# A layer's combination inside the second attention's loop, and a ternary layer's weight preparation moved ahead of the first experts

## The chip, the cores and the metric

The kernel runs on one core of a Trainium2 chip. The metric is device microseconds of one execution; the kernel before took 1500.44 us in the median of three runs (1497.56 to 1501.2). The core's engines are TensorE (PE), VectorE (DVE), ScalarE (ACT), GpSimd (POOL) and SyncE (SP, which here only starts DMAs). Each engine runs its own instructions in order and waits for others on semaphores.

## The reference

Four decoder layers on x of 64 x 64 x 128 float32 (4096 tokens, 32 tiles of 128 tokens x 128 features). Each layer has a cross-attention and a feed-forward part, both on a normalised x and both gated and added. The change touches the end of layer 0 and layer 1:

```
x = x + tanh(g_xattn[0]) * L0_xattn(layernorm(x), ctx, mask)      # 16 heads
x = x + tanh(g_ffn[0])   * L0_ffn(layernorm(x))                   # 16 experts, one per token
x = x + tanh(g_xattn[1]) * L1_xattn(layernorm(x), ctx, side)      # 16 heads, bias per head
x = x + tanh(g_ffn[1])   * L1_ffn(layernorm(x))                   # ternary weights

# L1_ffn: absmean(W) = sign(W/g) * min(round(|W/g|), 1), g = mean|W| + 1e-6
h = gelu(x @ absmean(W_fc).T)          # 128 -> 512
h = layernorm(h) * ln_w + ln_b
out = h @ absmean(W_proj).T            # 512 -> 128
```

"Combination" below is the second line's sum: the experts' output rows, times each token's gate, are added to x. Layers 2 and 3 follow and are not touched.

## The kernel before

x stays in SBUF as 32 tiles (core.x). The program is a sequence of phases; between phases all engines meet at a barrier. The functions return one program for each engine, and a phase queues them one behind another on that engine.

The phase `attentions_and_experts` holds three stages that follow each other without a barrier: `first` (attention of layer 0 with the router that sends each token's row to an expert's table in DRAM), `expert` (16 experts, each 256 rows: rows and weights are loaded, transposed, multiplied, and the results scattered to a table `rows_out`) and `second` (attention of layer 1). On PE and DVE the queue is first, expert, second; on SP too, with the rows of `rows_out` loaded into `got` by `FirstCombine.load_rows` after all results are stored.

Both attentions come from `attention16_programs`. Every engine runs a loop over i from -5, and a stage of the pipeline works on tile i plus some lead. For a tile: ACT normalises it (xn, L485) with rstd and nmr = -mean*rstd; PE transposes xn and projects q, k, v (L386 to L399); ACT copies them out (L500 to L508); POOL spreads kT into a block form kbd (L341), adds a shift to x (L357) and in the second attention adds the mask to the bias tile (side_add, L350); PE multiplies the scores (L413); DVE adds the bias to the scores (`masked`, L583), takes maxima (L590), subtracts them (`centred`, L598); ACT takes exponents (L515); PE transposes them (L428) and multiplies with v (L440); DVE divides (L607, L610), and after PE's output product (L454) adds to x (`residual`, L618) and takes bn_stats of the new x (L625). Buffers of kbd, xn and q are double; side tiles have four buffers; the scores have one.

The second attention gets `added`, a `FirstCombine`: before DVE's loop it calls `fresh(t)` for t = 0 to 31. fresh multiplies got by the gate and adds it to x (L1740, one instruction), takes bn_stats of the tile before (L1747), and after each group of 8 tiles runs `root_on_vector` (L199 to L219): 18 small DVE instructions that give mean, rstd (three Newton steps) and nmr of the group. ACT's xn of tile t waits for the nmr of its group. Only then does DVE enter its loop, whose first work is masked(0).

The next phase is `ternary_ffn` (l1f). SP loads W_fc, W_proj, ln_w and ln_b, then fills a table of layer 2 with empty rows (34 transfers, L1949). DVE computes the roots of all 32 tiles, and then prepares the weights: sums of absolute values (L2064), thresholds, signs (L2076 to L2079), gains and gate (L2081, L2083), and with PE's help (L1982, L1985, L1989) a shift and the correction for the mean (L2085, L2088). Then its loop over tiles starts with `normalise` (L2094).

Of the kernel before, what the change touches and what calls it, by code (L numbers as in the profile page):

```python
# [37 lines left out]
class Core:  # L38


    def __init__(self, nc, ctx):
# [10 lines left out]
        self.gates = sb("gates", [P, 8])  # L52
        self.tables = {}
# [131 lines left out]
def statistics(nc, ph, core, name="", groups=1):  # L185
# [8 lines left out]
    def on_vector(dve, group=0):  # L194
        V = nc.vector
        at = slice(group * NT // groups, (group + 1) * NT // groups)
        done = group * (8 + 3 * ROOT_STEPS)
# [23 lines left out]
        dve.wait_ge(nmr_ready, group + 1)  # L221
# [3 lines left out]
def attention16_programs(nc, core, ph, gate, w_dram, b_dram, neg_steps, side=None, fills=(), routing=None, added=None):  # L225
# [94 lines left out]
    def gpsimd(pool):  # L320
# [223 lines left out]
    def vector(dve):  # L544
# [3 lines left out]
        V.memset(fill_rows[:, :, 0:D], 0.0).then_inc(s["fill_ready"], 1)  # L548
        V.memset(fill_rows[:, :, D:ROW], NOWHERE).then_inc(s["fill_ready"], 1)
# [12 lines left out]
        def fresh(t):  # L562
# [1156 lines left out]
class FirstCombine:  # L1719
# [5 lines left out]
    def __init__(self, nc, core, ph, r):  # L1725
# [3 lines left out]
        self.s = {n: ph.sem(n) for n in ("added", "summed")}  # L1729
# [13 lines left out]
    def moments(self, dve, t):  # L1743
# [1415 lines left out]
```

## Time and profile before

| | us |
|---|---|
| median of three runs | 1500.44 (1497.56 to 1501.2) |
| the profiled execution's own time | 1497.47 |
| its span, first to last instruction | 1495.7 |
| PE busy (matmul) | 1155.3 (77%) |
| DVE busy | 986.8 (66%) |
| POOL busy | 834.0 (56%) |
| ACT busy | 788.1 (53%) |
| mean granted clock of TensorE | 0.892 of full |

Times in views are microseconds from the span's start. The stages that the change touches lie there as follows: first attention from about 27, experts from about 260, second attention from about 325, ternary layer from about 538 to 640. A timeline row has the start, the duration, the engine, the line, the operation, output<-inputs, a count, and in brackets how long the engine stood before it and what released it. Rows of consecutive instructions of one kind may be merged; then the duration is that of the merged piece.

### The profile page before, as it was taken

The page shows a single profiled execution, that of the slowest core. Times are in us where ns is not written, and L with a number is a line of the kernel's source. Part 1 is how long each engine was busy: PE and PEld are TensorE (multiplying, and loading weights), DVE is VectorE, ACT ScalarE, POOL GpSimd, SP SyncE. Part 2 cuts the span into 40 slices and gives each one's busy share as a digit, 9 for nine tenths or more (in the row PEclk, how much of TensorE's full clock was granted, in tenths as well). Part 3 has the DMA queues.
Part 4 walks back from the last instruction along what each step waited for, and adds up shares of the span by engine and source line. Part 5 has one row for each costly group of instructions (what it writes and reads, how often), then busy time and mean ns, then how long its engine had stood idle before and what let it go on. Part 6 is the DMA issues. An engine that isn't in the chain of part 4 may idle for free.

```text
span 1495.7 us, 38800 instructions
## 1 busy us (share of the span) xinstructions
PE 1155.3 (77%) x12350; PEld 974.5 (65%) x12350; DVE 986.8 (66%) x3128; ACT 788.1 (53%) x2054; POOL 834.0 (56%) x1103
## 2 busy tenths in 40 slices
PE   2888883962888859968529996698888973999991
PEld 1676662951767637736529996476666662999991
DVE  3788982239899957768834434588777864555554
ACT  2677761421788825545417776576555541433333
POOL 0356766442677703373764554677888874333334
PEclk9999995985899969987559999799999995999996
DMA  5222331570223257060116777200000301777765
GB/s 148 89 103 98 97 97 39 175 210 20 105 101 114 73 219 294 1 189 24 53 58 195 206 212 211 77 2 6 16 17 16 104 21 55 219 240 232 238 207 172
DMA packets 144386, 177.72 MB, mean 119 GB/s; under 512 B 18986, under 2 KB 94268, under 8 KB 144192
## 3 DMA queue, kind: packets, MB, share of 16 engines
q1 hardware_dynamic: 133504, 154.22, 33.1%
q0 software_dynamic: 10688, 21.06, 4.0%
q8 instruction: 105, 1.72, 0.5%
q14 instruction: 89, 0.73, 0.2%
HBM read 119.16 MB, written 57.23 MB: 118 GB/s over the span
## 4 chain that ended last, share of the span: by engine, by line
PE 31%; POOL 8%; DVE 7%; issue 6%; ACT 3%; DMA 2%; POOLq 0%; SPq 0%; DVEq 0%; ACTq 0%
PE l3e_ps_h L1604 4%; PE l2e_ps_h L1604 4%; PE l3e_ps_h L1606 4%; PE l3e_ps_y L1615 4%; PE l2e_ps_y L1615 4%; POOL l_rows_in L1178 3%; PE l3a_ps_kv L2628 2%; PE l3a_ps_ym L2699 2%; POOL l3a_cms L2521 1%; PE l3a_ps_q L2612 1%; DVE x L706 1%; POOL l3a_nvt L2538 1%; POOL l3a_qc L2529 1%; PE l3a_ps_kv L2603 1%; PE l3e_ps_x L1596 1%
## 5 line engine op out<-in xcount | busy, mean ns | idle before, releaser
L1645 ACT ACTIVATE l3e_sT<-l3e_ps_h 128x128 f32<-128x128 f32 x284 | 78.8, 278 | 134.2 <-PE l3e_ps_h L1606 121.3
L1698 POOL DMA_INDIRECT l_rows_out<-l3e_y,l3e_target x71 | 69.0, 972 | 137.8 <-DVE l3e_y L1680 133.7
L1656 DVE TENSOR_TENSOR l3e_hT<-l3e_sT,l3e_ps_h 128x128 f32<-128x128 f32 x284 | 81.7, 288 | 85.4 <-ACT l3e_sT L1645 75.8
L1642 ACT ACTIVATE l2e_hT<-l2e_ps_h,l2e_b1c 128x128 f32<-128x128 f32 x284 | 104.5, 368 | 56.1 <-PE l2e_ps_h L1604 39.8
L1604 PE MATMUL l2e_ps_h<-l2e_xT,l2e_w 128*128 128x128 f32 x568 | 111.0, 279 | 0.4 <-DVE l2e_xT L1669 0.4
L1604 PE MATMUL l3e_ps_h<-l3e_xT,l3e_w 128*128 128x128 f32 x568 | 111.0, 277 | 0.5 <-DVE l3e_xT L1669 0.5
L1606 PE MATMUL l3e_ps_h<-l3e_xT,l3e_w 128*128 128x128 f32 x568 | 110.6, 277 | 0.0
L1615 PE MATMUL l3e_ps_y<-l3w_w,l3e_hT 128*128 (+1 forms) x568 | 109.3, 275 | 0.0
L1615 PE MATMUL l2e_ps_y<-l2e_w,l2e_hT 128*128 (+1 forms) x568 | 109.2, 275 | 0.0
L1698 POOL DMA_INDIRECT l_rows_out<-l2e_y,l2e_target x71 | 69.1, 973 | 70.2 <-DVE l2e_y L1678 56.8
L1604 PEld LDWEIGHTS l3e_ps_h<-l3e_xT,l3e_w 128*128 128x128 f32 x568 | 87.1, 194 | 0.7 <-DVE l3e_xT L1669 0.7
L1604 PEld LDWEIGHTS l2e_ps_h<-l2e_xT,l2e_w 128*128 128x128 f32 x568 | 86.9, 194 | 0.9 <-DVE l2e_xT L1669 0.9
L1606 PEld LDWEIGHTS l3e_ps_h<-l3e_xT,l3e_w 128*128 128x128 f32 x568 | 87.1, 194 | 0.0
L1615 PEld LDWEIGHTS l2e_ps_y<-l2e_w,l2e_hT 128*128 128x128 f32 x568 | 86.1, 192 | 0.0
L1178 POOL DMA_INDIRECT l_rows_in<-l2a_rt_rows,l2f_slot x64 | 63.2, 988 | 40.9 <-ACT l2a_rt_rows L1020 23.2
L1615 PEld LDWEIGHTS l3e_ps_y<-l3w_w,l3e_hT 128*128 128x128 f32 x568 | 86.0, 192 | 0.1
L350 POOL TENSOR_TENSOR l1a_side<-l1a_side,l1a_neg 128x1024 f32<-128x1024 f32 x32 | 75.8, 2368 | 0.0
L1178 POOL DMA_INDIRECT l_rows_in<-l3a_rt_rows,l3f_slot x64 | 64.7, 1011 | 19.1 <-issue 17.4
L341 POOL TENSOR_TENSOR l1a_kbd<-l1a_kT,l1a_own 128x512 f32<-128x512 f32 x32 | 33.3, 1041 | 74.4 <-ACT l1a_kT L502 74.4
L341 POOL TENSOR_TENSOR l0a_kbd<-l0a_kT,l0a_own 128x512 f32<-128x512 f32 x32 | 34.5, 1077 | 56.5 <-ACT l0a_kT L502 56.2
L1966 POOL TENSOR_TENSOR l1f_rs<-l1f_ve,l1f_half 128x1 f32<-128x1 f32 x32 | 17.7, 552 | 66.6 <-DVE x L2113 45.5
L428 PE MATMUL l1a_ps_t<-ident,l1a_p 128*128 128x128 f32 x256 | 41.7, 288 | 16.2 <-ACT l1a_p L515 16.0
(551 smaller groups left out, 3766.4 us busy)
## 6 DMA issues: line engine op xcount, KB each, us to landing
l3e_w<-in_L_ffn_W SPq DMA_DIRECT2D x142, 256.0 KB
l2e_w<-in_L_ffn_w SPq DMA_DIRECT2D x79, 256.0 KB, 4.6
l_rows_in<-l1f_empty SPq DMA_DIRECT2D x34, 528.0 KB, 7.4
l1a_side<-in_fside_Bx16xSxS SPq DMA_DIRECT2D x32, 512.0 KB, 3.5
l0e_w<-in_L_ffn_w SPq DMA_DIRECT2D x32, 256.0 KB, 3.1
l_rows_in<-l0a_fill_rows SPq DMA_DIRECT2D x15, 528.0 KB, 2.7
l_rows_out<-l0a_fill_rows SPq DMA_DIRECT2D x12, 512.0 KB, 3.6
l2e_rows<-l_rows_in SPq DMA_DIRECT2D x71, 66.0 KB
```

Source lines behind the costliest of these rows:

```text
L341: pool.tensor_tensor(kbd[:, t % 2, :, :, :], kT[:, :, :].unsqueeze(2).broadcast_to([P, 2, HG, S]), own[:, :].unsqueeze(1).unsqueeze(3).bro ...
L350: pool.tensor_tensor(buf, buf, neg[:, t, :].unsqueeze(1).broadcast_to([P, H16, S]), ALU.add).then_inc(s["side_ready"], 1)
L428: last = nc.tensor.transpose(ps_t[:, j, :], p[:, 2 * j:2 * j + 2, :].rearrange("q a k -> q (a k)"), core.ident[:, :])
L1178: pool.indirect_dma_start(out=r.rows_in, out_offset=bass.IndirectOffsetOnAxis(ap=r.slot[:, k, t:t + 1], axis=0), in_=self.rows[:, t, k, :] ...
L1604: last = nc.tensor.matmul(ps_h[f][:, 0:SLOTS], w1[:, q % ROWS, f * P:f * P + P], xT[:, q % 2, :], start=True, stop=True)
L1606: last = nc.tensor.matmul(ps_h[f][:, SLOTS:2 * SLOTS], w3[:, q % ROWS, f * P:f * P + P], xT[:, q % 2, :], start=True, stop=True)
L1615: last = nc.tensor.matmul(ps_y[q % 2][:, 0:D], hT[:, q % 2, f, :], w2[:, columns(e, F, f * P, P)], start=(f == 0), stop=(f == FC - 1))
L1642: nc.scalar.activation(hT[:, q % 2, f, :], ps_h[f][:, 0:SLOTS], act_func, **bias).then_inc(sems["h_ready"], 1)
L1645: nc.scalar.activation(sT[:, f, :], ps_h[f][:, 0:SLOTS], act_func).then_inc(sems["s_ready"], 1)
L1656: nc.vector.tensor_tensor(hT[:, q % 2, f, :], sT[:, f, :], ps_h[f][:, SLOTS:2 * SLOTS], ALU.mult).then_inc(sems["h_ready"], 1)
L1698: pool.indirect_dma_start(out=r.rows_out, out_offset=bass.IndirectOffsetOnAxis(ap=target[:, q % RING:q % RING + 1], axis=0), in_=y[:, q % ...
L2628: nc.tensor.matmul(ps_kv[:, :], core.ctxT[:, t * P:(t + 1) * P], wkv[:, I:2 * I], start=True, stop=True).then_inc(s["v_ps"], 1)
```

## The change

Two things are done.

First, in the second attention DVE does only fresh(0) to fresh(7) before its loop; in its iterations i = -5 to -2 it does two tiles each (8 to 15) and in i = -1 to 14 one each (16 to 31). fresh no longer runs the root chain; it takes bn_aggr of each tile, two tiles behind the addition, and POOL computes the roots of a group of 8 with four instructions, one of them a power of -0.5 (`roots`): group 0 ahead of its loop, groups 1, 2 and 3 at the start of its iterations -1, 7 and 15. The memset of fill_rows is left out where there is nothing to fill.

Second, the preparation of the ternary weights becomes `ternary_weights`, a program of its own, with its own PSUM tile and with results in q_fc, w_out and w_shift of Core. Its loads are the first DMAs of the phase `attentions_and_experts` on SP; on DVE and PE it is queued between first and expert. The memset of ones moves from POOL to DVE, and PE's column sums now wait for the shift.

```
@@ attention16_programs
+    if added is None:
+        root_on_vector, nmr_ready = statistics(nc, ph, core)
+    else:
+        nmr_ready = added.s["nmr_ready"]
@@ gpsimd
+        if added is not None:
+            added.ready(pool)
+            added.roots(pool, 0)
         for i in range(-5, LAST):
+            if added is not None and i % added.GROUP == added.GROUP - 1:
+                added.roots(pool, (i + 1) // added.GROUP + 1)
             side_add(i + 3)
@@ vector
-        V.memset(fill_rows[:, :, 0:D], 0.0).then_inc(s["fill_ready"], 1)
-        V.memset(fill_rows[:, :, D:ROW], NOWHERE).then_inc(s["fill_ready"], 1)
+        if fills:
+            (the same two)
@@ fresh
             added.add(dve, t)
             added.moments(dve, t - 1 if t % added.GROUP > 0 else -1)
+            added.aggregate(dve, t - 2 if t % added.GROUP > 1 else -1)
             if t % added.GROUP == added.GROUP - 1:
                 added.moments(dve, t)
-                dve.wait_ge(added.s["summed"], t + 1)
-                root_on_vector(dve, t // added.GROUP)
+                added.aggregate(dve, t - 1)
+                added.aggregate(dve, t)
@@
-        for t in range(NT):
+        for t in range(8):
             fresh(t)
         for i in range(-5, LAST):
+            if i < -1:
+                fresh(2 * i + 18)
+                fresh(2 * i + 19)
+            else:
+                fresh(i + 17)
             outputs(i)
@@ FirstCombine
+    def aggregate(self, dve, t):
+        dve.wait_ge(self.s["summed"], t + 1)
+        self.nc.vector.bn_aggr(self.m[:, t, :], self.core.bn[:, t, :]).then_inc(self.s["aggregated"], 1)
+    def roots(self, pool, g):
+        s, at = self.s, slice(g * self.GROUP, (g + 1) * self.GROUP)
+        pool.wait_ge(s["aggregated"], (g + 1) * self.GROUP)
+        pool.tensor_scalar(self.veps[:, at], self.m[:, at, 1], LN_EPS, None, ALU.add).then_inc(s["root_steps"], 1)
+        pool.tensor_scalar(self.minus[:, at], self.m[:, at, 0], -1.0, None, ALU.mult).then_inc(s["root_steps"], 1)
+        pool.wait_ge(s["root_steps"], 3 * g + 2)
+        pool.tensor_tensor(self.core.rstd[:, at], self.veps[:, at], self.half[:, :], ALU.pow).then_inc(s["root_steps"], 1)
+        pool.wait_ge(s["root_steps"], 3 * g + 3)
+        pool.tensor_tensor(self.core.nmr[:, at], self.minus[:, at], self.core.rstd[:, at], ALU.mult).then_inc(s["nmr_ready"], 1)
@@ attentions_and_experts: sync | tensor | vector
+            ternary.sync(sp)
             first.sync(sp)
...
             first.tensor(pe)
             first_psum_free(pe)
+            ternary.tensor(pe)
             expert.tensor(pe)
             psum_free(pe)
+            ternary_psum_free(pe)
             second.tensor(pe)
...
             first.vector(dve)
+            ternary.vector(dve)
             expert.vector(dve)
@@ ternary_weights: tensor (new wait)
         pe.wait_ge(s["gated"], 1)
+        pe.wait_ge(s["shift_ready"], 1)
         for f in range(FC):
             last = nc.tensor.matmul(ps_w[:, 2 * P:2 * P + D], ones[:, :], w_out[:, f, :], ...)
```

The rest of `ternary_weights` has the instructions that left `ternary_ffn`, in their order.

## Rows read from the trace of the kernel before

**Rows 1.** Busy time by stretch, whole core: stretch, length, each engine's busy time (instructions), clock.
```profile
346.00:371.00 25.00, 4.10 (x31) 2.17 (x29) 23.53 (x84) 2.81 (x9) 9.15 (x7) 0.50 0.00 0
537.00:554.00 17.00, 4.34 (x18) 3.99 (x18) 10.83 (x35) 1.28 (x1) 1.20 (x4) 0.53 0.86 319
554.00:640.00 86.00, 83.30 (x480) 60.18 (x480) 58.49 (x191) 46.17 (x96) 31.21 (x64) 0.95 0.41 160
```

**Rows 2.** Timeline, start of the second attention; columns as explained above.
```profile
333.47 0.61 DVE L1740 SCALAR_TENSOR_TENSOR x<-l0c_got,l0f_weight,x 128x128 f32<-128x128 f32 x2 [1.45 <-DMA l0c_got<-l_rows_out]
...
337.24 0.17 DVE L199 TENSOR_TENSOR l1a_gap<-bn 128x8 f32<-128x8 f32 x1
...
340.45 0.49 ACT L485 ACTIVATE l1a_xn<-x,nmr,rstd 128x128 f32<-128x128 f32 x1 [17.87 <-DVE nmr L219]
...
346.19 1.16 PE L413 MATMUL l1a_ps_s<-l1a_kbd,l1a_qT 32*64 32x256 f32 x16
...
370.44 1.22 DVE L583 SCALAR_TENSOR_TENSOR l1a_s<-l1a_side,l1a_ps_s 128x1024 f32<-128x1024 f32 x1
```

**Rows 3.** Timeline, one period of the second attention's steady loop.
```profile
422.18 1.22 DVE L583 SCALAR_TENSOR_TENSOR l1a_s<-l1a_side,l1a_ps_s 128x1024 f32<-128x1024 f32 x1
...
422.73 2.36 POOL L350 TENSOR_TENSOR l1a_side<-l1a_side,l1a_neg 128x1024 f32<-128x1024 f32 x1
...
424.90 1.27 DVE L598 TENSOR_TENSOR l1a_s<-l1a_s,l1a_mx 128x1024 f32<-128x1024 f32 x1
...
425.87 0.36 ACT L502 ACTIVATE l1a_kT<-l1a_ps_a,l1a_bias 128x128 f32<-128x128 f32 x1
...
426.31 1.04 POOL L341 TENSOR_TENSOR l1a_kbd<-l1a_kT,l1a_own 128x512 f32<-128x512 f32 x1 [1.22 <-ACT l1a_kT L502]
...
426.49 0.26 DVE L607 RECIPROCAL l1a_rden<-l1a_ps_b 128x16 f32<-128x16 f32 x1 [0.32 <-PE l1a_ps_b L440]
...
427.17 1.22 DVE L583 SCALAR_TENSOR_TENSOR l1a_s<-l1a_side,l1a_ps_s 128x1024 f32<-128x1024 f32 x1
```

**Rows 4.** Timeline, start of the ternary layer.
```profile
538.67 0.33 SPq L1941 DMA_DIRECT2D l1f_wfc<-in_L_ffn_W_fc  x1
...
540.54 22.43 SPq L1949 DMA_DIRECT2D l_rows_in<-l1f_empty  x19
...
542.68 0.69 DVE L2064 TENSOR_REDUCE l1f_sums<-l1f_wfc 128x1 f32<-128x512 f32 x1
...
551.21 1.91 PE L1989 MATMUL l1f_ps_y<-l1f_w_out,l1f_ones 128*128 128x128 f32 x8
...
553.77 0.59 DVE L2094 TENSOR_SCALAR l1f_xn<-x,mean,rstd 128x128 f32<-128x128 f32 x2
```

**Rows 5.** Timeline, start of the first attention.
```profile
34.68 0.77 PE L376 MATMUL l0a_ps_b<-l0a_w,l0a_bias 128*128 128x128 f32 x2 [8.82 <-DMA l0a_bo<-in_L_xattn_bo]
...
35.92 0.49 ACT L485 ACTIVATE l0a_xn<-x,nmr,rstd 128x128 f32<-128x128 f32 x1 [7.42 <-DVE l0a_bias L554]
```

**Rows 6.** Timeline, between the first attention and the experts.
```profile
250.48 0.32 DVE L1249 TENSOR_SCALAR l0f_weight<-l0a_rt_wsum,gates 128x32 f32<-128x32 f32 x1
...
259.54 0.66 PE L1378 MATMUL l0e_ps_x<-ident,l0e_rows 128*128 128x128 f32 x2 [12.70 <-DMA l0e_rows<-l_rows_in]
```

**Rows 7.** Powers of four and one column on POOL; bn_aggr: duration ns min/median/max.
```profile
201.60 1.04 POOL L1003 TENSOR_TENSOR l0a_rt_rstd<-l0a_rt_small 128x4 f32<-128x4 f32 x1
...
L1966 POOL TENSOR_TENSOR l1f_rs<-l1f_ve,l1f_half x32: 548/550/608, 559.1 to 636.7; 128x1 f32<-128x1 f32 x32
...
L2103 DVE BATCH_NORM_AGGREGATE l1f_mv<-l1f_bn x32: 181/182/183, 558.6 to 635.9; 128x2 f32<-128x6 f32 x32
```

**Rows 8.** Timeline, a stretched DVE instruction beside POOL's; L706: duration ns min/median/max.
```profile
345.38 2.35 POOL L350 TENSOR_TENSOR l1a_side<-l1a_side,l1a_neg 128x1024 f32<-128x1024 f32 x1
...
345.49 2.27 DVE L203 SCALAR_TENSOR_TENSOR l1a_gap<-l1a_gap 128x8 f32<-128x8 f32 x1
...
L706 DVE SCALAR_TENSOR_TENSOR x<-l3c_got,l3f_weight,x x32: 337/535/539, 1473.6 to 1488.2; 128x128 f32<-128x128 f32 x32
```

More of the change, by code:

```diff
@@ L192, in statistics, with on_vector @@
     stepped, nmr_ready = ph.sem(f"{name}stepped"), ph.sem(f"{name}nmr_ready")
-    def on_vector(dve, group=0):
+    def on_vector(dve):
         V = nc.vector
-        at = slice(group * NT // groups, (group + 1) * NT // groups)
-        done = group * (8 + 3 * ROOT_STEPS)
+        at, done = slice(0, NT), 0
         even, odd = core.bn[:, at, 1], core.bn[:, at, 4]
@@ L547, in vector @@
             root_on_vector(dve)
[L548 to L549 removed]
+        if fills:
+            V.memset(fill_rows[:, :, 0:D], 0.0).then_inc(s["fill_ready"], 1)
+            V.memset(fill_rows[:, :, D:ROW], NOWHERE).then_inc(s["fill_ready"], 1)
         dve.wait_ge(s["w_in"], 64)
@@ L774, in attentions_and_experts @@
         expert, all_stored, psum_free, _ = expert_programs(nc, core, part, r, 16, 1, a["L0_ffn_w1"], a["L0_ffn_w2"], ACT.Relu)
+        ternary_part = Part(phase, "l1w", "right")
+        ternary, ternary_psum_free = ternary_weights(nc, core, ternary_part, 5, a["L1_ffn_W_fc"], a["L1_ffn_W_proj"], a["L1_ffn_ln_w"], a["L1_ffn_ln_b"])
+        ternary_part.release_psum()
         part.release_psum()
@@ L1728, in __init__ @@
         self.arrived = [ph.sem(f"rows_arrived{g}") for g in range(self.NG)]
-        self.s = {n: ph.sem(n) for n in ("added", "summed")}
+        self.m, self.half = ph.sb("moments", [P, NT, 2]), ph.sb("half", [P, self.GROUP])
+        self.veps, self.minus = ph.sb("veps", [P, NT]), ph.sb("minus", [P, NT])
+        self.s = {n: ph.sem(n) for n in ("added", "summed", "aggregated", "filled", "root_steps", "nmr_ready")}
     def load_rows(self, sp):
@@ L1913, in ternary_ffn @@
+def ternary_ffn(nc, core, name, table):
+    F = core.q_fc.shape[1]
+    FC = F // P
+    with Phase(nc, name) as ph:
+        q_fc, w_out, shift = core.q_fc, core.w_out, core.w_shift
         half = ph.sb("half", [P, 1])
@@ L1954, in _ @@
         def _(pool):
-            pool.memset(ones[:, :], 1.0).then_inc(s["filled"], 1)
             pool.memset(half[:, :], -0.5).then_inc(s["filled"], 1)
@@ L1979, in _ @@
         def _(pe):
-            pe.wait_ge(s["filled"], 2)
-            pe.wait_ge(s["summed0"], 2)
-            nc.tensor.matmul(ps_y[0][:, 0:2], ones[:, :], sums[:, :], start=True, stop=True).then_inc(s["sums_ps"], 1)
-            pe.wait_ge(s["quantised"], 3)
-            for f in range(FC):
-                last = nc.tensor.matmul(ps_y[0][:, 0:D], lnb[:, f:f + 1].broadcast_to([P, P]), q_proj[:, f, :], start=(f == 0), stop=(f == FC - 1))
-            last.then_inc(s["shift_ps"], 1)
-            pe.wait_ge(s["gated"], 1)
-            for f in range(FC):
-                last = nc.tensor.matmul(ps_y[1][:, 0:D], ones[:, :], w_out[:, f, :], start=(f == 0), stop=(f == FC - 1))
-            last.then_inc(s["col_ps"], 1)
-            pe.wait_ge(s["shift_ready"], 1)
-            pe.wait_ge(s["folded"], 1)
             @for_tile
```

132 lines of the change are left out of this document (78 added, 54 removed).

## The prediction

> **What bounds the kernel now.** I read the busy table by stage first, since no engine bounds the whole. From 346 to 371 us DVE is busy 23.53 of 25 us while PE does 4.10; from 537 to 554 PE does 4.34 of 17; from 554 to 640 it does 83.30 of 86 [rows 1]. So the stretches that the change aims at are two in which PE waits for DVE, and the ternary layer's loop behind the second is PE's own.
>
> The timeline gives their lengths. Second attention: the first combination starts at 333.47, the first group's root chain at 337.24, the first xn on ACT at 340.45, the first scores on PE at 346.19, but the first masked addition (L583) only at 370.44: DVE finishes all four groups before it [rows 2]. Steady loop: 427.17 - 422.18 = 4.99 us a tile, in which DVE stands 0.32 before the reciprocal and about 0.1 elsewhere, so some 4.6 us are work [rows 3]. Ternary layer: the roots end where the first weight reduction starts, 542.68, and the first xn is at 553.77 [rows 4].
>
> **Ternary layer (gain 11.1).** All that stands between these two rows leaves: 553.77 - 542.68 = 11.1 us. Nothing else is late there, since the first xn needs mean and rstd alone. SP's table fill starts earlier by the four issues that leave, and goes on beside PE's loop, as now. Bounds: 10 to 12.
>
> **Its four loads, now first on SP (loss 1.9).** Their issues take 540.54 - 538.67 = 1.9 us [rows 4], and they now stand ahead of the first attention's weight and bias loads. There PE waited 8.82 us for the last of these, and ACT's first xn stood 7.42 us [rows 5]: nothing hides it, and the whole first attention moves. 512 KB more in flight could add up to 1; I take 1.9, bounds 1.8 to 3.
>
> **The preparation between attention and experts (loss 2.5).** DVE ends its part of the first attention at 250.48 + 0.32 = 250.8; PE's first expert instruction is at 259.54, when its rows land [rows 6]. The hole is 8.7 us, the preparation longer. In its present place it takes 551.21 - 542.68 = 8.5 us from the first reduction to PE's column sums, and these 1.91 [rows 4]. A new wait of PE for the scaled shift ahead of them costs an estimated 0.6, because the shift is computed from the product that PE ends just before. With 0.2 for the moved memset, PE is free for experts at 250.8 + 0.2 + 8.5 + 0.6 + 1.9 = 262.0, against 259.54: 2.5 late. Queued behind PE's waits is the first transposition of rows, and all experts wait for it; the rows are no cover, as both sides move by the 1.9 above. Bounds 0 (the rows themselves come that much later, and hide it) to 3.5.
>
> **Second attention, the start (gain 22.6).** Before masked(0) DVE will do 16 combinations, not 32, and no root chain. Eight now take 337.24 - 333.47 = 3.8 us, the chain 340.45 - 337.24 = 3.2 [rows 2]. After: 3.8, plus eight bn_aggr, each of 0.18 duration but about 0.09 in line as they overlap (0.7 together), then POOL's four instructions. Of these the power is long: 0.55 us for one column, 1.04 for four [rows 7], so about 1.7 for eight (bounds 1.04 and 2.1); with three small ones and their waits 2.5. 3.8 + 0.7 + 2.5 = 7.0, as now, and xn(0) stays at 340.5. Scores(0) end at 346.19 + 1.16 = 347.4 [rows 2], POOL's first side addition at 345.38 + 2.35 = 347.7 [rows 8]; DVE's tiles 8 to 15 (8 x 0.54) fit in before. Masked(0) comes at about 347.8 in place of 370.4. The memset of fill_rows that goes stood in a wait of DVE for POOL: nothing.
>
> **The price in the loop (loss 16.3).** For tiles 16 to 31 one iteration carries one combination: add, bn_stats and bn_aggr, in line 0.25 + 0.20 + 0.09 = 0.54 us. 4.6 + 0.54 = 5.1, just over the present period, so DVE becomes the loop's bound. Then contention decides. A DVE operation on SBUF inputs that meets a running POOL operation ends with it: one of 128x8, 0.17 us elsewhere, took 2.27, from 345.49 to 347.76, and POOL's side addition ran from 345.38 to 347.73. L706, the same form and size as the new add, takes 337 ns at its shortest and 535 in the median, beside POOL's additions [rows 8]. In the loop kT is ready at 425.87 + 0.36 = 426.23 and POOL's kbd starts at 426.31, while DVE's centred subtraction (two SBUF inputs) runs from 424.90 to 426.17 [rows 3]. Once DVE lags by 0.2 us, kbd (1.04 us) is already waiting when centred ends and is let in ahead of the add, which then stands about 0.8. Period 5.0 + 0.8 = 5.8, that is 0.8 more than now; over the 13 iterations after start-up 10.4. POOL's roots of groups 2 and 3 wait for nothing (their moments are an iteration old), but queued behind their 2.5 us is a side addition that now ends at 422.73 + 2.36 = 425.1 and is needed at 427.17 [rows 3], and kbd behind it: about 2 us each time, 4. The start-up, where banked work is missing (side additions and kbd done during the 25 us) and DVE carries tiles 8 to 15 as well: 1.9. Sum 10.4 + 4 + 1.9 = 16.3, and the stage gains 22.6 - 16.3 = 6.3. Bounds of the price: 2.4 (no stall, roots hidden: 16 x 0.15) and 39.5 (each add behind a side addition, below).
>
> One rule speaks to the stall. In the Trainium skill, "SBUF — State Buffer", section "Who interferes with whom", issue order decides who blocks, and the winner keeps the port pair for its whole instruction. The stretched operations of this trace agree. By that rule an add issued right behind centred and ahead of kbd is the winner; whether a POOL instruction that already waits for centred is let in before DVE's next one, it does not say. If DVE's next one is, the first rival comes true.
>
> **Sum.** -11.1 + 1.9 + 2.5 - 22.6 + 16.3 = -13.0. The profiled execution took 1497.47 us (span 1495.7 and 1.8 around it), so 1484.5; the median of the runs lies 3.0 higher, so 1487 against 1500.44. A change under 0.3% (4.5 us) can't be told from none.
>
> **Rivals.** The add goes first (0.16): POOL yields and the period stays near 5.14. For it: POOL stands idle before kbd today. Against it: L706's median, which shows strict taking of turns. Loop price 2.4, stage -20.2, total -26.9: 1473.5.
>
> POOL becomes the drag (0.12): roots and stretched kbd delay the scores, and the period is 6.15 over 16 iterations, 0.35 more each. Against: POOL's three operations are 3.9 us of 4.99 now (kbd 1.04, x shift about 0.46, side addition 2.36). 5.6 more: stage -0.7, total -7.4: 1493.
>
> The add behind the side addition (0.04), the slower case: if DVE falls behind kbd's start by more than 1.5 us (kbd 1.04 and the x shift after it), the add meets the side addition of 2.36 and stands 2.1. 16 x 2.1 + 5.9 = 39.5 against 22.6: stage +16.9, total +10.2: 1510.6. Against: a DVE that late also delays its own o, and with it kT and the side addition.
>
> That the preparation is hidden after all (the hole between attention and experts grows by itself) would be 1484.5, within the forecast.
>
> **Numbers.** The forecast holds 0.66, with its own range 1482 to 1492. With the first two rivals the range for 8 in 10 is 1472 to 1495; 0.02 is left for nothing changed by much. Faster 0.91, same 0.05 (half from the tail of the second rival), slower 0.04 (the third).
>
> **What would show it.** Right: the first L583 near 348 to 350; L583's distances 5.8 for tiles 4 to 16 and 4.99 from tile 20; new adds of 1.1 us beside kbd of 1.4; the first ternary xn 4 us after its phase begins; the first expert transposition 11 us after DVE's last instruction of the first attention; the first l0a xn 1.9 later. Wrong: adds of 0.33 throughout the loop, distances of 7, the experts' start unmoved against DVE's end, masked(0) after 355.

## The result, and the profile after

The changed kernel takes 1481.06 us in the median of four runs (1480.06 to 1483.02), the kernel before 1499.67 on the same chip: ratio 0.9878, 95% interval 0.9861 to 0.9896, or 18.6 us less. Forecast were 13.0 less, to 1487; 1481.06 lies 0.9 us below the forecast's own range (1482 to 1492) and inside its wider one (1472 to 1495). The profiled execution took 1480.96 us, 16.5 less than that of before.

The page of the changed kernel, its first lines: PE is busy for 5 us more than before, and DVE's busy time has fallen by 12.

```profile
span 1478.9 us, 38676 instructions
...
PE 1160.6 (78%) x12350; PEld 978.2 (66%) x12350; DVE 974.7 (66%) x3087; ACT 788.5 (53%) x2054; POOL 849.4 (57%) x1119
```

Busy time by stretch, changed kernel; columns as in [rows 1]. The 25 us that follow upon the start of the second attention now have PE busy for 20.10, and in the ternary layer the 86 us of PE's own loop come 3.7 us behind the start of the phase.

```profile
351.00:376.00 25.00, 20.10 (x240) 14.96 (x239) 21.06 (x28) 14.13 (x36) 21.87 (x17) 0.72 0.24 86
530.00:535.00 5.00, 0.14 (x1) 0.14 (x1) 3.80 (x20) 1.28 (x1) 1.10 (x3) 0.50 0.48 193
535.00:621.00 86.00, 83.08 (x480) 60.03 (x480) 58.65 (x191) 46.18 (x96) 31.22 (x64) 0.96 0.51 205
```

Timeline of the changed kernel, in the order of the program: start of the first attention [rows 5], between attention and experts [rows 6], start of the second attention [rows 2], one period of its loop [rows 3], start of the ternary layer [rows 4]. L1764 is the addition, L593 the masked addition, L608 centred, L620 o (the divided values), L344 kbd.

```profile
37.63 0.49 ACT L493 ACTIVATE l0a_xn<-x,nmr,rstd 128x128 f32<-128x128 f32 x1 [8.43 <-DVE l0a_bias L563]
...
252.26 0.32 DVE L1271 TENSOR_SCALAR l0f_weight<-l0a_rt_wsum,gates 128x32 f32<-128x32 f32 x1
...
262.23 2.04 PE L1973 MATMUL l1w_ps_w<-w_out,l1w_ones 128*128 128x128 f32 x8 [0.54 <-DVE w_shift L2002]
...
264.07 0.63 PE L1400 MATMUL l0e_ps_x<-ident,l0e_rows 128*128 128x128 f32 x2
...
338.28 0.61 DVE L1764 SCALAR_TENSOR_TENSOR x<-l0c_got,l0f_weight,x 128x128 f32<-128x128 f32 x2 [1.44 <-DMA l0c_got<-l_rows_out]
...
343.49 1.67 POOL L1792 TENSOR_TENSOR rstd<-l0c_veps,l0c_half 128x8 f32<-128x8 f32 x1
...
345.56 0.49 ACT L493 ACTIVATE l1a_xn<-x,nmr,rstd 128x128 f32<-128x128 f32 x1 [18.51 <-POOL nmr L1794]
...
352.82 1.22 DVE L593 SCALAR_TENSOR_TENSOR l1a_s<-l1a_side,l1a_ps_s 128x1024 f32<-128x1024 f32 x1 [5.95 <-POOL l1a_side L353]
...
425.42 1.33 DVE L608 TENSOR_TENSOR l1a_s<-l1a_s,l1a_mx 128x1024 f32<-128x1024 f32 x1
...
426.38 0.36 ACT L510 ACTIVATE l1a_kT<-l1a_ps_a,l1a_bias 128x128 f32<-128x128 f32 x1
...
426.68 0.34 DVE L1764 SCALAR_TENSOR_TENSOR x<-l0c_got,l0f_weight,x 128x128 f32<-128x128 f32 x1
426.82 1.09 POOL L344 TENSOR_TENSOR l1a_kbd<-l1a_kT,l1a_own 128x512 f32<-128x512 f32 x1 [1.16 <-ACT l1a_kT L510]
...
427.22 0.22 DVE L617 RECIPROCAL l1a_rden<-l1a_ps_b 128x16 f32<-128x16 f32 x1
427.48 0.29 DVE L620 TENSOR_TENSOR l1a_o<-l1a_ps_b,l1a_rden 128x128 f32<-128x128 f32 x1
427.69 1.22 DVE L593 SCALAR_TENSOR_TENSOR l1a_s<-l1a_side,l1a_ps_s 128x1024 f32<-128x1024 f32 x1
...
530.72 0.21 DVE L199 TENSOR_TENSOR l1f_gap<-bn 128x32 f32<-128x32 f32 x1 [1.73 <-PEq L80]
...
534.46 0.60 DVE L2157 TENSOR_SCALAR l1f_xn<-x,mean,rstd 128x128 f32<-128x128 f32 x2
```

Two things are to be seen in the loop's rows. The new addition takes 0.34 us and stands 0.14 us ahead of kbd, not behind it as I had forecast. And DVE has next to no idle time left, yet the next masked addition is at 432.68, again 4.99 us on.

Stage by stage, one trace against the other:

| | before | after | moved by | forecast |
|---|---|---|---|---|
| first xn of the first attention | 35.92 | 37.63 | +1.71 | +1.9 |
| DVE's last of the router to first expert transposition | 9.06 | 11.81 | +2.75 | +2.5 |
| first combination to masked(0) | 36.97 | 14.54 | -22.43 | -22.6 |
| masked(0) to masked(31) | 156.28 | 165.81 | +9.53 | +16.3 |
| ternary phase's first DVE instruction to its first xn | 15.05 | 3.74 | -11.31 | -11.1 |

These make -19.75, and the next phase's first DVE instruction moves from 641.80 to 621.98, by 19.82. From there to the end nothing was changed; that part took 853.9 us before and 856.9 after. The 3.0 are scatter: the same part takes between 852.4 and 857.8 in the traces of e2 to e8 below, and 849.8 in that of e1.

The loop's price of 9.53 lies in few places. The distances from one masked addition to the next were, in the changed kernel, 5.67 6.35 6.39 5.82, then 4.99 4.99 4.99 5.33 5.38 7.63 7.48 4.86, then 4.99 4.99 4.99 5.36 4.73 6.46 5.07 4.73 4.96, then 4.99 to the end. Before they were 3.82 7.75 5.24 5.00, then 4.99. So the start-up costs 2.4 more, the region of group 2's roots 5.7, that of group 3's 1.4, and each other iteration nothing. In the two regions, 0.34 and 0.37 us belong to the distances 5.33 and 5.36: there a group ends, and DVE takes one bn_stats and two bn_aggr more.

### The profile page after: what moved, and what is told of

Same layout as the page of the kernel before. It is cut to its first block, busy times and chain, and to the rows that moved or that the text cites. A ratio compares the mean times of both kernels' runs of the same rounds, so it can differ in the third digit from the quotient of the medians.

```text
span 1478.9 us, 38676 instructions
## 1 busy us (share of the span) xinstructions
PE 1160.6 (78%) x12350; PEld 978.2 (66%) x12350; DVE 974.7 (66%) x3087; ACT 788.5 (53%) x2054; POOL 849.4 (57%) x1119
## 4 chain that ended last, share of the span: by engine, by line
PE 33%; POOL 8%; issue 6%; DVE 6%; ACT 3%; DMA 2%; POOLq 0%; SPq 0%; DVEq 0%; ACTq 0%
PE l3e_ps_h L1626 4%; PE l3e_ps_h L1628 4%; PE l3e_ps_y L1637 4%; PE l2e_ps_h L1626 4%; PE l2e_ps_y L1637 4%; POOL l_rows_in L1200 2%; PE l3a_ps_kv L2689 2%; PE l3a_ps_ym L2760 2%; PE l3a_ps_q L2673 1%; POOL l3a_cms L2582 1%; POOL x L714 1%; POOL l3a_nvt L2599 1%; PE l3a_ps_o L2748 1%; POOL l3a_qc L2590 1%; DMA l_rows_out<-l2e_y,l2e_target 1%
## 5 line engine op out<-in xcount | busy, mean ns | idle before, releaser
L353 POOL TENSOR_TENSOR l1a_side<-l1a_side,l1a_neg 128x1024 f32<-128x1024 f32 x32 | 75.8, 2368 | 0.0
L344 POOL TENSOR_TENSOR l0a_kbd<-l0a_kT,l0a_own 128x512 f32<-128x512 f32 x32 | 34.9, 1091 | 56.0 <-ACT l0a_kT L510 55.7
L344 POOL TENSOR_TENSOR l1a_kbd<-l1a_kT,l1a_own 128x512 f32<-128x512 f32 x32 | 37.9, 1185 | 36.2 <-ACT l1a_kT L510 36.2
L1494 POOL DMA_INDIRECT l_rows_out<-l0e_y,l0e_target x32 | 31.1, 973 | 43.8 <-DVE l0e_y L1482 38.9
```

The lines of the kernel that those rows point to most:

```text
L344: pool.tensor_tensor(kbd[:, t % 2, :, :, :], kT[:, :, :].unsqueeze(2).broadcast_to([P, 2, HG, S]), own[:, :].unsqueeze(1).unsqueeze(3).bro ...
L353: pool.tensor_tensor(buf, buf, neg[:, t, :].unsqueeze(1).broadcast_to([P, H16, S]), ALU.add).then_inc(s["side_ready"], 1)
L1494: pool.indirect_dma_start(out=r.rows_out, out_offset=bass.IndirectOffsetOnAxis(ap=target[:, c % 2, a:a + 1], axis=0), in_=y[:, c % 2, a, : ...
```

## Experiments

Each is a kernel of its own, in five rounds against the kernel before on the same chip; ratios, not times, are compared, since one of the chips runs everything some 28 us slower. Loop is the time from masked(0) to masked(31) in the trace. "Ordinary" are distances away from start-up and group ends.

| kernel | ratio to before (95%) | loop | ordinary distances |
|---|---|---|---|
| before | 1 | 156.28 | 4.99 |
| changed | 0.9878 (0.9861 to 0.9896) | 165.81 | 4.99 |
| e1 ternary alone | 0.9968 (0.9950 to 0.9986) | 154.31 | 4.99 |
| e2 combination alone | 0.9935 (0.9905 to 0.9965) | 168.60 | 5.64, later 4.99 |
| e3 roots spread | 0.9890 (0.9857 to 0.9922) | 163.48 | 4.99, later 5.64 |
| e4 roots behind side | 0.9906 (0.9876 to 0.9937) | 168.34 | 4.99, later 5.64 |
| e5 one bn_stats more | 0.9907 (0.9873 to 0.9941) | 171.83 | 5.04, later 5.84 |
| e6 two bn_stats more | 0.9934 (0.9908 to 0.9960) | 173.85 | 5.31 and 6.03 in turns |
| e7 loads later | 0.9873 (0.9846 to 0.9899) | 167.33 | 5.64, later 4.99 |
| e8 sums after experts | 0.9861 (0.9834 to 0.9888) | 165.80 | 4.99 |
| e9 kbd waits | 0.9886 (0.9856 to 0.9917) | 166.74 | 4.99 to 5.30 |
| e10 kbd waits, spread | 0.9838 (0.9810 to 0.9865) | 163.53 | 5.30 |
| e11 all | 0.9826 (0.9798 to 0.9855) | 163.50 | 5.30 |
| e12 addition behind o | 0.9831 (0.9807 to 0.9855) | 162.42 | 4.99 |

### e1 and e2: each half alone

e1 is the kernel before with `ternary_weights`, e2 the kernel before with the new `fresh`, `aggregate` and `roots`.

> The kernel before with the second half of the change alone (the ternary weights prepared between first attention and first experts; the combination stays ahead of the second attention's loop). Theory (parts add up, as the trace of the changed kernel has them): ternary layer -11.3, loads first on SP +1.0, preparation +2.75, so -7.5 us against before, about 1492. Rival (the preparation's cost is larger when measured alone, because the start of the program, 0.7 later in the changed kernel's trace, belongs to it too): -6.8. My terms on record give -6.7. The first expert transposition comes 11.8 us after DVE's last router instruction, the first ternary xn 3.7 after its phase's first DVE instruction.

> The kernel before with the first half of the change alone (combination of tiles 8 to 31 in the second attention's loop, roots on POOL; the ternary layer prepares its own weights). Theory: -22.4 at the start and +9.5 in the loop, so -12.9 us, about 1487; together with the other half -20.4, or 1.8 more than the changed kernel gains, which its trace shows as time lost behind the ternary layer. Rival (my terms on record: +16.3 in the loop): -6.3. Rival 2 (the halves help each other): the two gains sum to less than 18.6.

e1: 0.9968, which is 4.8 us of 1496.75 (2.1 to 7.5). The interval includes the 6.8 and 6.7 and just reaches the 7.5 expected. The places came out as expected: the first expert transposition at 264.15, 11.81 behind DVE's last router instruction at 252.34, and the first ternary xn at 544.84, 3.81 behind its phase's first DVE instruction at 541.03. e2: 0.9935, 9.7 us (5.2 to 14.2). I had expected 12.9, from a loop of 9.5 more; its loop took 168.60 - 156.28 = 12.3 more, and 22.4 - 12.3 = 10.1 fits the runs. The interval also includes the rival's 6.3, so it is the loop's 12.3, not the total, that speaks against a price of 16.3. The two halves come to 14.5, with an uncertainty that includes the 18.6; neither rival of a joint effect is shown. What is new stands in e2's distances: 5.97 5.65 5.64 5.63 6.03, for tiles where the changed kernel had 5.82 4.99 4.99 4.99 5.33. The DVE and POOL programs of that loop are the same in both. What sets off the slower rhythm there was not found.

### e3 and e4: where the roots of groups 2 and 3 stand

In e4 the call moves behind the side addition; in e3 it is cut there into `roots_part`, with parts 0 (the two small operations), 1 and 2 (powers of four columns) and 3 (nmr) in four iterations. Group 1 stays as it was.

```diff
@@ gpsimd (e4)
-            if added is not None and i % added.GROUP == added.GROUP - 1:
-                added.roots(pool, (i + 1) // added.GROUP + 1)
             side_add(i + 3)
+            if added is not None and i > 0 and i % added.GROUP == added.GROUP - 1:
+                added.roots(pool, (i + 1) // added.GROUP + 1)
             spread(i + 4)
@@ gpsimd (e3)
             side_add(i + 3)
+            if added is not None and i >= 7 and (i - 7) % 8 < 4:
+                added.roots_part(pool, (i + 1) // added.GROUP + 1, (i - 7) % 8)
             spread(i + 4)
```

> The changed kernel, with POOL's roots of groups 2 and 3 cut into four pieces (two small operations, two powers of four columns, one small operation), one piece per iteration, in the gap of 1.2 us that POOL has between side addition and kbd. xn(16) needs them four iterations after they can start. Theory A (the 2.5 us of roots ahead of a side addition make it late, PE starves for 2.9 us and its granted clock falls): 7.1 us in the loop, of which 5.5 to 7 come back; masked distances near 4.99 from tile 4 to 31, clock 1.00 throughout; 1475 against 1481. Theory B (the loss at tiles 9 to 12 is due to the double bn_stats and bn_aggr on DVE at the group's end and the adds that then meet kbd): at most 2 us come back, the distances of 7.5 stay.

> The changed kernel, with POOL's roots of groups 2 and 3 whole (2.5 us), but behind the iteration's side addition, ahead of kbd, in place of ahead of both. Theory A (late side addition is what costs): the side addition is in time, kbd comes 2.5 - 1.2 = 1.3 us late; one iteration each of 1.3 more, clock not lost: 4.5 us better than the changed kernel, about 1476.5. Theory A2 (any lateness of POOL makes PE stand and costs the clock): no better than 2 us. Theory B (DVE's double statistics cost it): no change, 1481.

Neither brought anything in the runs: e3's loop is 2.3 us shorter than the changed kernel's, where theory A had 5.5 to 7, and e4's is 2.5 longer. What the place costs in the changed kernel is seen in its timeline (first fence) and windows (second):

```profile
403.37 1.67 POOL L1792 TENSOR_TENSOR rstd<-l0c_veps,l0c_half 128x8 f32<-128x8 f32 x1
...
405.27 2.35 POOL L353 TENSOR_TENSOR l1a_side<-l1a_side,l1a_neg 128x1024 f32<-128x1024 f32 x1
405.44 3.27 DVE L608 TENSOR_TENSOR l1a_s<-l1a_s,l1a_mx 128x1024 f32<-128x1024 f32 x1
407.59 2.02 POOL L344 TENSOR_TENSOR l1a_kbd<-l1a_kT,l1a_own 128x512 f32<-128x512 f32 x1
408.63 1.12 DVE L1764 SCALAR_TENSOR_TENSOR x<-l0c_got,l0f_weight,x 128x128 f32<-128x128 f32 x1
...
410.50 0.48 PE L456 MATMUL l1a_ps_b<-ident,l1a_o 128*128 128x128 f32 x1 [2.89 <-DVE l1a_o L620]
```

```profile
404.00:409.00 5.00, 3.50 (x66) 2.56 (x64) 5.00 (x5) 2.70 (x8) 4.92 (x4) 1.00 0.31 107
409.00:419.00 10.00, 8.51 (x78) 7.49 (x79) 7.50 (x16) 5.33 (x13) 6.63 (x6) 0.51 0.15 55
```

The side addition behind the roots meets centred, which is held to 3.27 us; PE stands 2.89, its granted clock falls to 0.51 for ten us (the lower level, 1.2 GHz), and two periods of 7.5 follow. In e3 both are gone: there the clock is 1.00 from 400 to 420 us, and no distance over 6.03 is left in that region. So theory A had the cause of this loss right. But its gain was given back: from group 2's end on the distances are 5.57 5.64 5.64 5.63 5.64 5.64 6.03. Trace of e3, window and timeline (L1766 is the addition):

```profile
400.00:420.00 20.00, 17.01 (x279) 12.88 (x277) 19.90 (x34) 15.36 (x38) 16.88 (x17) 1.00 0.32 108
```

```profile
418.27 1.29 POOL L344 TENSOR_TENSOR l1a_kbd<-l1a_kT,l1a_own 128x512 f32<-128x512 f32 x1 [0.60 <-ACT l1a_kT L512]
418.58 1.13 DVE L1766 SCALAR_TENSOR_TENSOR x<-l0c_got,l0f_weight,x 128x128 f32<-128x128 f32 x1
```

This is the stall of my forecast: kbd first, the addition 1.13 us. In e4 the whole roots ahead of kbd took longer than thought (the power 2.48 us beside centred), and kbd came at 412.45. The lateness then passed on to the next side addition, which met centred after all, one iteration later; L353 is the side addition, L610 centred:

```profile
413.86 2.36 POOL L353 TENSOR_TENSOR l1a_side<-l1a_side,l1a_neg 128x1024 f32<-128x1024 f32 x1
414.04 3.26 DVE L610 TENSOR_TENSOR l1a_s<-l1a_s,l1a_mx 128x1024 f32<-128x1024 f32 x1
```

PE stood 2.82 us, its clock was 0.66 from 419 to 424, one distance was 7.68, and the slower rhythm followed. So theory A had the collision right and its price for e4 (1.3 us, no clock lost) wrong; A2's total came true, by the same collision.

### e5 and e6: more work for DVE in the loop

e6 has range(2).

```diff
             added.moments(dve, t - 1 if t % added.GROUP > 0 else -1)
+            if t >= 2 * added.GROUP:
+                for k in range(1):
+                    V.bn_stats(added.spare[:, k, t, :], core.x[:, t - 1, :])
```

> The changed kernel with one bn_stats more (same form, result unused) behind each of the additions of tiles 16 to 31 in the loop, 0.20 us in line. Test of the step that I priced at 10.4: once DVE is the bound, POOL's kbd is let in ahead of the next add. In the changed kernel DVE's work just fits in 4.99. Theory C (my mechanism is right, only its condition was not met): with 0.2 more DVE falls behind, the add stands 0.8, distances of 5.8 in the ordinary iterations, total 8 to 10 us more, about 1490. Theory D (no overtaking: the work just adds up): distances near 5.15 and 2 to 3 us more, 1484. Theory E (there is slack beyond the 0.2): no change, 1481.

> As the run before, with two bn_stats more per addition, 0.40 us in line. Theory C: a step and then a plateau, distances 5.8 to 6.0, about 1491. Theory D: distances 5.35, 5 to 6 us more, about 1487. Theory E (slack of about 0.3): 1.5 more.

Both C and D occur. In e5, one after the other: the distances are 5.13 5.05 5.05 between tiles 4 and 7 and 5.85 5.83 5.83 between tiles 12 and 15. In e6 in turns: 5.31 6.04 6.02, later 5.31 6.03. The loops are 6.0 and 8.0 us longer than the changed kernel's, between D's forecasts (2 to 3, and 5 to 6) and C's (8 to 10, and 10). Two neighbouring iterations of e5 show the two cases; L1768 is the addition:

```profile
424.78 0.34 DVE L1768 SCALAR_TENSOR_TENSOR x<-l0c_got,l0f_weight,x 128x128 f32<-128x128 f32 x1
424.81 1.22 POOL L344 TENSOR_TENSOR l1a_kbd<-l1a_kT,l1a_own 128x512 f32<-128x512 f32 x1 [1.21 <-ACT l1a_kT L510]
425.99 1.21 DVE L596 SCALAR_TENSOR_TENSOR l1a_s<-l1a_side,l1a_ps_s 128x1024 f32<-128x1024 f32 x1
...
429.79 1.04 POOL L344 TENSOR_TENSOR l1a_kbd<-l1a_kT,l1a_own 128x512 f32<-128x512 f32 x1 [1.03 <-ACT l1a_kT L510]
429.82 1.15 DVE L1768 SCALAR_TENSOR_TENSOR x<-l0c_got,l0f_weight,x 128x128 f32<-128x128 f32 x1
...
431.84 1.21 DVE L596 SCALAR_TENSOR_TENSOR l1a_s<-l1a_side,l1a_ps_s 128x1024 f32<-128x1024 f32 x1
```

Which of two instructions is 0.03 us ahead decides over 0.8 us. Over four additions of e5 (tiles 20 to 23) the lead on kbd shrank from 0.19 to 0.14, 0.08 and 0.03, each of them still 0.34 to 0.35 long. The fast rhythms also give DVE's real need. With 0.2 more the period was 5.05, with next to no idle time on DVE and centred at its free 1.22: 5.05 - 0.2 = 4.85. With 0.4 more it was 5.31, of which centred was held for 0.06 (it took 1.27): 5.31 - 0.4 - 0.06 = 4.85. So DVE needs some 4.85 us, and 0.14 of the 4.99 is slack.

### e7 and e8: the ternary layer's two costs

```diff
@@ sync (e7)
-            ternary.sync(sp)
-            first.sync(sp)
+            first.sync(sp, between=ternary.sync)
@@ tensor (e8): ternary_sums is PE's last loop of ternary_weights
             expert.tensor(pe)
             psum_free(pe)
+            ternary_sums(pe)
             ternary_psum_free(pe)
@@ vector (e8): ternary_fold is its last DVE instruction
             expert.vector(dve)
+            ternary_fold(dve)
```

> The changed kernel with the four ternary loads not first on SP, but after the first attention's own loads (at its fourth tile). Theory: the 1.0 us at the first xn comes back, 1480. Rival (my 1.9 on record, of which 0.9 was hidden by chance): 1.9 back, 1479. Rival 2: they delay the router's loads or table fills instead: no change.

> The changed kernel with the ternary preparation cut: PE's column sums (2.04 us) and DVE's fold (0.69) are queued behind the experts, ahead of the second attention, where PE and DVE wait for the rows of the combination. What stays between attention and experts ends with PE's shift product at 261.7 in the trace; the rows land at about 261.3. Theory: 2.3 of the 2.75 us come back, 1478.7. Rival (PE's later start of its bias product delays DVE's weight scaling and own, hence POOL and the first side additions): part of it is lost again, 1480.

Neither total can be told from the changed kernel's; the places can. The trace of e7 (PE's wait for bo, then first xn):

```profile
34.52 0.77 PE L384 MATMUL l0a_ps_b<-l0a_w,l0a_bias 128*128 128x128 f32 x2 [7.75 <-DMA l0a_bo<-in_L_xattn_bo]
...
35.76 0.49 ACT L493 ACTIVATE l0a_xn<-x,nmr,rstd 128x128 f32<-128x128 f32 x1 [6.35 <-DVE l0a_bias L563]
```

One pair of traces misled me here. From the phase's first DVE instruction (a root's) to the first xn, the nine traces of kernels with the loads in front have 9.60 to 10.56 us, mean 9.80; the five without have 8.66 (before), 7.61, 7.60, 7.71 and 7.52, mean 7.82. The loads cost 2.0, as forecast. The trace of before was the late one of its kind, and that is why the pair showed 1.0 beside a phase that began 0.7 later by chance.

In e8 the way from DVE's last router instruction to the first transposition is 9.20 us in place of 11.81, so 2.6 of the 2.75 are back. Before it was 9.06, so next to nothing of the preparation is left exposed. Nothing is lost again behind the experts, as the rival had it: from the first combination to masked(0) it is 14.54 us, as in the changed kernel. In the trace of e8 the transposition follows PE's shift product without a gap:

```profile
262.54 2.07 PE L1970 MATMUL l1w_ps_w<-l1w_q_proj,l1w_lnb 128*128 128x128 f32 x8 [4.92 <-DVE w_out L2002]
...
264.41 0.63 PE L1402 MATMUL l0e_ps_x<-ident,l0e_rows 128*128 128x128 f32 x2
```

e7's loop had four distances of 5.64 (from masked(3) to masked(7)), though its loop's code is the changed kernel's. One iteration of it, beside that of the changed kernel shown first; L1763 is the addition:

```profile
386.98 1.22 DVE L608 TENSOR_TENSOR l1a_s<-l1a_s,l1a_mx 128x1024 f32<-128x1024 f32 x1
...
387.37 0.36 ACT L510 ACTIVATE l1a_kT<-l1a_ps_a,l1a_bias 128x128 f32<-128x128 f32 x1
...
387.80 1.29 POOL L344 TENSOR_TENSOR l1a_kbd<-l1a_kT,l1a_own 128x512 f32<-128x512 f32 x1 [1.56 <-ACT l1a_kT L510]
388.11 1.13 DVE L1763 SCALAR_TENSOR_TENSOR x<-l0c_got,l0f_weight,x 128x128 f32<-128x128 f32 x1
...
389.91 1.21 DVE L593 SCALAR_TENSOR_TENSOR l1a_s<-l1a_side,l1a_ps_s 128x1024 f32<-128x1024 f32 x1
```

In the changed kernel centred began at 425.42, inside POOL's side addition, and the addition was ahead of kbd by 0.14. Here centred began late enough to run free of the side addition (1.22 for 1.33), kT was ready at 387.73 while centred still ran, and kbd had been queued before the addition's turn came. Whether the later loads delay the first attention itself (rival 2) stays open: from its first to its last masked addition it took 181.9 us in e7 and 182.0 in e11, the longest of all traces, but 177.7 in e12, which has the same order of loads.

### e9, e10 and e11: the order forced

```diff
@@ spread(t), ahead of kbd (e9)
+            if added is not None and 4 <= t < 18:
+                pool.wait_ge(added.s["added"], t + 15)
```

e10 adds to this the roots of groups 1, 2 and 3 in four parts, as in e3; e11 adds to e10 the edits of e7 and e8.

> The changed kernel with one wait more: POOL's kbd of tiles 4 to 17 waits for the combination that DVE has queued at that place (kbd(t) for the addition of tile t + 14), so the addition always goes first. What the runs so far left: the loop has two rhythms, 4.99 with an addition of 0.34 ahead of kbd, and 5.64 with one of 1.13 behind it, and the same code falls into either (4 distances of 5.64 in the run with later loads, none in the changed kernel's own trace). Theory F (the order of these two decides): no distance of 5.64 is left, no addition over 0.4 from tile 19 on; the loop takes 164 to 166 with the roots still ahead of the side addition, as in the changed kernel's good trace; 1481. Theory G (the rhythm comes from elsewhere, a late PE or clock): distances of 5.64 stay, or the wait itself costs 0.2 each, 2 to 3 more.

> As the run before, with the roots of groups 1, 2 and 3 in four pieces over four iterations behind the side addition. With the spread alone the group ends kept the loop at 5.64 for six tiles. Theory F: now the spread pays; no distance over 5.5 from tile 4 on, loop 158 to 160 in place of 165.8, total about 1475. Theory G: loop 163 or more.

> As the run before, with the ternary loads behind the first attention's own (worth 1.85: first xn 7.96 behind its phase's start in three traces without them in front, 9.81 in seven with) and the column sums and fold behind the experts (2.6 by the trace). If all three add up: 6 + 1.9 + 2.6 = 10.5 less than the changed kernel, about 1470.5; if the preparation's saving is lost in the first attention's own scatter of times, 1473.

From tile 17 on every addition takes 0.34 us, and no distance of 5.64 with an addition behind kbd is left: the order of these two does decide that rhythm. But the forced order has a period of its own, 5.30, between the two free ones, which e9 reaches after two or three tiles and e10 keeps. The trace of e10 shows why; L355 is the side addition, L610 centred, L1766 the addition, L346 kbd:

```profile
387.92 2.37 POOL L355 TENSOR_TENSOR l1a_side<-l1a_side,l1a_neg 128x1024 f32<-128x1024 f32 x1
...
389.71 1.66 DVE L610 TENSOR_TENSOR l1a_s<-l1a_s,l1a_mx 128x1024 f32<-128x1024 f32 x1
...
391.29 0.34 DVE L1766 SCALAR_TENSOR_TENSOR x<-l0c_got,l0f_weight,x 128x128 f32<-128x128 f32 x1
...
391.80 1.04 POOL L346 TENSOR_TENSOR l1a_kbd<-l1a_kT,l1a_own 128x512 f32<-128x512 f32 x1 [1.52 <-PE l1a_ps_s L423]
```

The profile names PE for kbd's wait; the scores happen to end with the addition. It is the addition that kbd waits for: kbd starts 0.17 us behind its end in each of e10's iterations without root pieces, also in the one from 403.29, where the scores end only 0.22 after kbd's start. kbd now starts 0.51 behind the addition's start, not 0.14, so the next side addition comes later too and holds centred for 1.66 us instead of 1.33. e9 alone therefore gains nothing (loop 166.7, where theory F had 164 to 166). With the roots spread as well the loop is 163.5: theory G's "163 or more" and not F's 158 to 160, since eight distances between masked(3) and masked(16) are 5.4 to 5.7, at the group ends and the roots, and 5.7 and 6.3 follow at group 3's roots; centred took up to 2.58 there. In the runs e10 stands 0.5% better than e9, and at the 1475 that was expected of it (0.9838), but the loops differ by 3.2 us only; where the rest of the 9 us between the medians comes from isn't shown. e11 is at 0.9826, 1.74% under before; the 1470.5 expected would have been 0.9806 of 1499.67, and its rival's 1473 0.9822, and the interval includes both.

### e12: the addition elsewhere

```diff
-            else:
-                fresh(i + 17)
+            elif added is not None:
+                added.moments(dve, i + 16 if i + 16 < NT else -1)
+                added.aggregate(dve, i + 15 if i + 15 < NT else -1)
             outputs(i)
+            if added is not None and -1 <= i < NT - 17:
+                added.add(dve, i + 17)
             masked(i + 2)
```

Loads and sums stand as in e11; kbd's wait is out; the roots are in three parts, without double statistics at the ends of groups 1 to 3.

> The changed kernel with the loads later and the sums behind the experts as in the run before, without the wait of kbd, and the in-loop combination placed otherwise: bn_stats and bn_aggr of the tiles before stand ahead of the reciprocal (in the 0.3 us that DVE waits there), the addition behind o and ahead of masked, no double statistics at the ends of groups 1 to 3, roots in pieces over three iterations behind the side addition. Theory H (the 5.64 rhythm and the 5.30 of the ordered kernel both come from an addition between centred and o, which delays o or kbd): o is not delayed, the addition meets at most kbd's last 0.3 us; distances 5.1 to 5.4 and no second rhythm, loop 160 to 162 against 163.5 of the run before, ratio to before 0.981. Theory I (DVE is the bound in any order and an addition between o and masked meets kbd or the x shift in full, 0.8 us): distances 5.6 to 5.9, loop 168 or more, ratio 0.986.

The timeline of e12 (L609 centred, L1776 bn_stats, L618 reciprocal, L1769 the addition, L594 masked):

```profile
426.76 1.21 DVE L609 TENSOR_TENSOR l1a_s<-l1a_s,l1a_mx 128x1024 f32<-128x1024 f32 x1
427.90 0.28 DVE L1776 BATCH_NORM_STATS2 bn<-x 128x6 f32<-128x128 f32 x1
...
427.93 1.04 POOL L344 TENSOR_TENSOR l1a_kbd<-l1a_kT,l1a_own 128x512 f32<-128x512 f32 x1 [1.16 <-ACT l1a_kT L511]
...
428.64 0.48 DVE L1769 SCALAR_TENSOR_TENSOR x<-l0c_got,l0f_weight,x 128x128 f32<-128x128 f32 x1
429.04 1.21 DVE L594 SCALAR_TENSOR_TENSOR l1a_s<-l1a_side,l1a_ps_s 128x1024 f32<-128x1024 f32 x1
```

Theory H holds for the ordinary iterations, and better than it said: kbd starts at once, the addition meets only its tail and takes 0.48, the period is 4.99, and neither rhythm, 5.64 or 5.30, occurs. Its loop of 160 to 162 was just missed: 162.42. What is left above 156.28 lies in distances of 5.4 to 6.4 at the start-up and at the roots, where centred is held up to 2.72. The double statistics and the number of root pieces were changed together with the place, so the 1.1 us between this loop and e11's isn't the place's alone. The ratio, 0.9831, can't be told from e11's. Both intervals end at 0.9855, just below that of the changed kernel, which starts at 0.9861, so either beats both kernels.

## Why the prediction was right, and which step of it was not

**Ternary layer, -11.1.** Right: -11.3. The two reductions, signs, sums and waits were all that stood there [rows 4].

**Loads first on SP, +1.9.** Right as a mean over 14 traces, 2.0. The pair of traces alone would have corrected it to 1.0, wrongly.

**Preparation, +2.5.** Right: 2.75. PE waited for the scaled shift 0.54 us where I had put 0.6, and the first transposition followed its sums at once. e8 shows that the sums and the fold were nearly all that was exposed: with them moved 2.6 come back.

**Second attention, start, -22.6.** Right: -22.43. The first xn came 7.28 behind the first combination, where it had been 6.98 and I had put 7.0; the power of eight columns took 1.67, for an estimate of 1.7.

**The price in the loop, +16.3.** Wrong in its largest term: 9.53 in the changed kernel's trace. The start-up was 2.4 for 1.9, the two roots 7.1 for 4. The third term, 10.4 for thirteen iterations in which kbd overtakes the addition, was 0 in the ordinary iterations. The step that failed is "once DVE lags by 0.2 us": there it did not lag, because its work was over-sized. I had taken 4.6 of the 4.99 us for work, counting only 0.32 and about 0.1 as waiting, and added 0.54. One more row of the kernel before, o, shows what that missed:

```profile
426.79 0.29 DVE L610 TENSOR_TENSOR l1a_o<-l1a_ps_b,l1a_rden 128x128 f32<-128x128 f32 x1
```

Start to start, from centred to the reciprocal it was 426.49 - 424.90 = 1.59 us, where a centred that nobody holds gives way after 1.13 (388.11 - 386.98 in e7's rows); from the reciprocal to o 0.30, in the changed kernel 0.26; from o to the masked addition 427.17 - 426.79 = 0.38, there 0.21. So 0.46 + 0.04 + 0.17 = 0.67 us of the period was waiting: the idle time, the 0.06 for which the side addition (422.73 to 425.09) held centred, and the 0.08 or so by which rows without a wait overlap. That leaves 4.32 of work, and with 0.54 it makes 4.86, as e5 measures (4.85), and not 5.14. So the loop kept its 4.99, with the addition 0.14 us ahead of kbd.

The mechanism itself is there, with nearly the price I had put on it. An addition behind kbd took 1.13 us where I had put 1.1, and the period was 5.64 where I had put 5.8 (4.85 and 0.8 make 5.65; the sum on record adds the 0.8 to 5.0, and with its own 5.14 would have given 5.9). This loop code falls into that rhythm in some traces and not in others: four iterations in e7, three in e2 (and two at 6.0), none in the changed kernel's own and in e8. Even there four of the sixteen additions took 1.12 to 1.13, those of tiles 16 and 18 in the start-up and 24 and 25 behind the group's end, so the stall is also a part of the other two terms. The first rival ("the add goes first", period near 5.14) described the ordinary iterations of this one trace better than my forecast, but its total of -26.9 failed on the roots and the start-up: 9.53 is far from its 2.4. The second and third rivals did not occur.

The roots' term had the late side addition, but not what it met. In the changed kernel it held centred for 3.27 us, PE stood, and the clock fell for ten us; and the double statistics at the two group ends (0.34 and 0.37) were in no term.

My question of what comes first when a POOL instruction already waits for centred is answered by e7 and e3: POOL's, in every one of those iterations. In the Trainium skill, "SBUF — State Buffer", section "Who interferes with whom", issue order decides who blocks. The traces agree: wherever an addition and a kbd overlap, the one whose row starts first has its way, down to a lead of 0.03 us (e5). The addition that starts 0.14 us ahead of kbd takes 0.34, and the one 0.31 behind takes 1.13.

**The sum.** -13.0 forecast, -16.5 in the profiled execution, -18.6 in the medians. The loop's term gives 6.8 more gain than forecast, and 3.0 of scatter behind the ternary layer hide a part of it. That the total came so near is in part luck: of the 10.4 that did not occur, 3.6 were made up by the start-up and the roots, which I had put too low, and 3.0 by the scatter.

## What to carry to other kernels

Before adding work to an engine that looks nearly full, measure its work from start to start in rows that wait for nothing, and not as the period less the idle time that is printed: an instruction that starts inside another engine's instruction and runs longer than its neighbours is in part a wait, though it is shown as busy. Where two engines' instructions hold each other up and come within 0.2 us of each other, a loop can have two rhythms. Forcing the order with a semaphore had a price of its own here (5.30 against 4.99); placing the new instruction where it meets only the end of the other kept 4.99, though the two kernels' totals can't be told apart. And read a cost of 1 to 2 us at one place over several traces of kernels that share that place, not from one pair.

## What the runs showed of the hardware that I had not expected

- The same loop code (changed kernel, e2, e7, e8) ran at 4.99 or 5.64 us a tile, and changed from one to the other at a disturbance (a group's end, the roots), not by itself. With more work on DVE (e5, e6) it changed within a group too.
- POOL's power of eight columns, 1.67 us, did not hold DVE: the three additions beside it, from 343.80 to 345.15, took 0.31 each. Its side addition and kbd, with 1024 and 512 columns, did. The other way round the power was held: behind a centred that was already running it took 2.48 (e4).
- The first attention, whose loop no kernel changes, took 175.9 to 182.0 us from its first to its last masked addition. In four of the first ten traces single distances of 7.5 stood in it that the others lack, between tiles 19 and 26. This scatter is larger than several of the effects studied; its cause stays open.
- On one chip (e9 to e11) the kernel before took 1527.27 us, at a granted clock of 0.875 to 0.893, against 0.884 to 0.897 in its runs on the other chips. In the traces from there the experts of layer 0 took 75.6 to 77.6 us from the first transposition to the first combination, against 72.8 to 74.8 elsewhere, and the part behind the ternary layer 872 to 879, against 850 to 858, so most of the 28 us lies there. Why was not tried.
